# One barrier per stage, earlier gathers in the mixture with capacity, and mixture sums written into the output tensor

## The reference

```python
C = int(CAP_FACTOR * S / E)                      # 160 rows for each expert
h = relu(einsum('ecd,edh->ech', xin, w1) + b1)   # xin: the rows picked for expert e
out = einsum('ech,ehd->ecd', h, w2) + b2
final = zeros.at[idx.reshape(-1)].add(out * weight)
```

```python
x = x + _L3_ffn_ref(_layernorm(x, axis=-1), L3_ffn_Wg, L3_ffn_bg, ...)
return x
```

## Time and profile before

| | us |
|---|---|
| median of 3 runs (lowest, highest) | 1863.27 (1859.93, 1864.88) |
| the profiled execution's own time | 1854.92 |
| its span, first to last instruction | 1852.8 |
| mean granted clock of TensorE | 0.939 |

### The profile page before, as it was taken

One profiled execution on the slowest core, in us unless ns is written; L12 is line 12 of the kernel. 1 busy time (PEld: TensorE's weight loads), 2 busy tenths in 40 slices (PEclk: granted clock), 3 DMA queues, 4 the chain that ended last, 5 costly groups with the idle time before them and its releaser, 6 DMA issues. The chain is left out here.

```text
span 1852.8 us, 35956 instructions
## 1 busy us (share of the span) xinstructions
PE 1617.7 (87%) x12777; PEld 1376.1 (74%) x12777; DVE 1109.5 (60%) x3057; ACT 817.1 (44%) x2383; POOL 792.2 (43%) x934
## 2 busy tenths in 40 slices
PE   6999999766887999987899999969959888859997
PEld 5899989634556999965798889845648745548996
DVE  5888786468854888845666766728951132363331
ACT  4766666213324888831666666620003212113332
POOL 7656656253337999833111111116732420102332
PEclk9999999789897999998999999989969989979998
DMA  8554554200013343302533333251036285761222
GB/s 257 176 169 152 175 164 153 79 1 1 1 28 121 137 139 124 130 18 90 162 107 113 115 106 114 82 187 36 1 103 205 30 210 138 253 218 36 37 40 46
DMA packets 139520, 206.20 MB, mean 111 GB/s; under 512 B 21410, under 2 KB 107106, under 8 KB 138706
## 3 DMA queue, kind: packets, MB, share of 16 engines
q1 hardware_dynamic: 131922, 194.07, 32.8%
q0 software_dynamic: 6720, 8.79, 3.0%
q10 hardware_dynamic: 704, 1.05, 0.2%
HBM read 163.53 MB, written 42.19 MB: 111 GB/s over the span
## 5 line engine op out<-in xcount | busy, mean ns | idle before, releaser
L810 DVE TENSOR_SCALAR xattn_oT<-bank,xattn_last 128x256 f32<-128x256 f32 x256 | 111.8, 478 | 91.7 <-PE bank L631 91.7
L716 ACT ACTIVATE xattn_probs<-bank,xattn_negmax 128x257 f32<-128x257 f32 x256 | 123.7, 483 | 65.5 <-DVE xattn_negmax L791 65.4
L721 ACT ACTIVATE xattn_probs<-xattn_probs,xattn_rsum 128x257 f32<-128x257 f32 x256 | 131.9, 515 | 1.4 <-DVE xattn_rsum L795 1.4
L1036 POOL TENSOR_SCALAR xattn_probs<-xattn_probs,xattn_rsum 128x257 f32<-128x257 f32 x128 | 119.5, 933 | 23.6 <-DVE xattn_rsum L1273 23.5
L791 DVE TENSOR_REDUCE xattn_negmax<-bank 128x1 f32<-128x257 f32 x256 | 106.5, 416 | 34.8 <-PE bank L604 33.2
L800 DVE TENSOR_TENSOR xattn_probsT_lo<-bank,xattn_probsT_hi 128x256 fp32r<-128x256 f32 x256 | 105.1, 410 | 9.8 <-ACT xattn_probsT_hi L727 8.7
L611 PE MATMUL bank<-ident,xattn_probs 128*128 128x128 f32 x512 | 103.9, 285 | 7.0 <-ACT xattn_probs L721 6.5
L147 ACT COPY xnT<-bank 128x512 f32<-128x512 f32 x40 | 21.4, 590 | 200.6 <-PE bank L137 200.6
L727 ACT CAST xattn_probsT_hi<-bank 128x256 fp32r<-128x256 f32 x256 | 95.4, 373 | 32.3 <-PE bank L611 28.2
L549 POOL COPY ctx_stat<-xattn_mv 128x2 f32<-128x2 f32 x32 | 6.0, 188 | 237.9 <-DVE xattn_mv L824 237.9
L600 PE MATMUL bank<-xattn_ctxT,xattn_qk_hi 128*128 128x258 f32 x256 | 93.8, 367 | 0.5 <-DVE xattn_qk L787 0.5
(11 more groups left out here) (488 smaller groups left out, 5332.6 us busy)
## 6 DMA issues: line engine op xcount, KB each, us to landing
xattn_ctxT<-ctx_partsT SPq DMA_DIRECT2D x64, 516.0 KB, 4.0
xattn_ctxN<-ctx_partsN SPq DMA_DIRECT2D x64, 384.0 KB, 4.2
ctx_partsT<-xattn_ctxT SPq DMA_DIRECT2D x32, 516.0 KB, 2.6
moe_w<-in_L_ffn_W SPq DMA_DIRECT2D x16, 1024.0 KB, 12.9
ctx_partsN<-xattn_ctxN SPq DMA_DIRECT2D x32, 384.0 KB, 3.5
moecap_w_early<-in_L_ffn_w SPq DMA_DIRECT2D x10, 1024.0 KB, 9.3
xattn_rawN<-in_ctx SPq DMA_DIRECT2D x32, 192.0 KB, 2.7
xattn_raw<-in_ctx SPq DMA_DIRECT2D x32, 192.0 KB, 4.3
```

Source lines behind the costliest of these rows:

```text
L716: nc.scalar.activation(probs[:, n % RING, :], SB[n % 2][:, 0:KV], ACT.Exp, bias=negmax[:, n % RING:n % RING + 1], accum_out=psum[:, n % RI ...
L721: nc.scalar.mul(probs[:, n % RING, :], probs[:, n % RING, :], rsum[:, n % RING:n % RING + 1]).then_inc(norm_ready, 1)
L810: nc.vector.tensor_scalar(oT[k][:, heads, b, :], by_head(OB[:, k * 2 * P:(k + 1) * 2 * P]), last[:, k, j * PER_TILE + b:j * PER_TILE + b + ...
L1036: nc.gpsimd.tensor_scalar(probs[:, n % RING, :], probs[:, n % RING, :], rsum[:, n % RING:n % RING + 1], None, ALU.mult).then_inc(norm_read ...
```

## The change

Three edits.

1. The second barrier of a stage's end goes. Instead, the semaphore numbers of the ended stage rest for one more stage: they are cleared by POOL, reserved again under new names, and released only when the following stage has ended. So a number comes into use again only after another block's barrier has passed.
2. In the mixture with capacity POOL issues one gather more ahead of its sums: gathers 0 to 3 first, then gather(n + 4) and add(n).
3. The last mixture's sums are accumulated in the output tensor itself, which is made P = 128 rows longer (the spare rows of padding; the host takes the first 1024). The eight copies and the wait for them go. SP still waits for all sums.

```diff
     def end(self):
-        self.core.nc.clear_and_free_semaphores(self.sems)
-        self.core.nc.all_engine_barrier()
+        core, nc = self.core, self.core.nc
+        nc.clear_and_free_semaphores(self.sems)
+        for rested in core.resting:
+            nc.release_semaphore(rested)
+        core.resting = [nc.alloc_semaphore(f"{self.name}_rests{k}", num=sem.num) for k, sem in enumerate(self.sems)]
...
-        self.sum = nc.dram_tensor(f"{name}_sum", (TOKENS + spare, D), F32, kind="Internal").ap()
+        self.sum = sums if sums is not None else nc.dram_tensor(f"{name}_sum", (TOKENS + spare, D), F32, kind="Internal").ap()
...
-            for n in range(XS):
+            for n in range(XS + 1):
                 gather(n)
             for n in range(E):
-                if n + XS < E:
-                    gather(n + XS)
+                if n + XS + 1 < E:
+                    gather(n + XS + 1)
                 add(n)
...
-        self.rows = Rows(core, ctx, "moe", self.E, P)
+        self.rows = Rows(core, ctx, "moe", self.E, P, core.out)
...
-        def put_out(eng, tiles):
-            for z in range(YS):
-                eng.wait_ge(y_added[z], 16 * len(range(z, BLOCKS, YS)))
-            for t in tiles:
-                eng.dma_start(out[t * P:(t + 1) * P, :], rows.sum[t * P:(t + 1) * P, :]).then_inc(put, 16)
...
-            put_out(sp, range(0, TILES, 2))
-            sp.wait_ge(put, TILES * 16)
+            for z in range(YS):
+                sp.wait_ge(y_added[z], 16 * len(range(z, BLOCKS, YS)))
...
-            put_out(act, range(1, TILES, 2))
...
-    out = nc.dram_tensor("out_0_dram", (BATCH, SEQ, D), F32, kind="ExternalOutput").ap()
+    out = nc.dram_tensor("out_0_dram", (TOKENS + P, D), F32, kind="ExternalOutput").ap()
```

More of the change, by code:

```diff
@@ L30, in __init__ @@
         self.nc, self.dram = nc, dram
+        self.resting = []
         self.x = ctx.enter_context(nc.sbuf_tensor("x", [P, TILES, D], F32))
@@ L2378, with __init__ @@
 class Rows:
-    def __init__(self, core, outer, name, experts, spare):
+    def __init__(self, core, outer, name, experts, spare, sums=None):
         nc = core.nc
@@ L2777, in stage_moe @@
         y_added = [st.sem(f"y_added{k}") for k in range(YS)]
-        put = st.sem("put")
         steps = st.sem("dve_steps")
         block = ctx.enter_context(nc.Block())
-        out = core.out.rearrange("b s n -> (b s) n")
         def expert_of(eng, n):
             return eng.value_load(expert_u[0:1, n:n + 1], min_val=0, max_val=E - 1)
-        def put_out(eng, tiles):
-            for z in range(YS):
-                eng.wait_ge(y_added[z], 16 * len(range(z, BLOCKS, YS)))
-            for t in tiles:
-                eng.dma_start(out[t * P:(t + 1) * P, :], rows.sum[t * P:(t + 1) * P, :]).then_inc(put, 16)
         @block.sync
@@ L3506 @@
         dram[name] = nc.dram_tensor(f"in_{name}", a.shape, _mybir.dt.from_np(a.dtype), kind="ExternalInput").ap()
-    out = nc.dram_tensor("out_0_dram", (BATCH, SEQ, D), F32, kind="ExternalOutput").ap()
+    out = nc.dram_tensor("out_0_dram", (TOKENS + P, D), F32, kind="ExternalOutput").ap()
     program(nc, dram, out)
     r = _run(nc, [arrays], core_ids=[0])
-    return r.results[0]["out_0_dram"]
+    return r.results[0]["out_0_dram"][0:TOKENS].reshape(BATCH, SEQ, D)
```

## The result

| | before | after |
|---|---|---|
| median of 4 runs each, us (lowest, highest) | 1861.77 (1859.93, 1864.88) | 1829.39 (1827.55, 1832.97) |
| ratio, 95% interval | | 0.9827 (0.9803 to 0.985) |
| the profiled execution's own time | 1854.92 | 1831.08 |
| its span | 1852.8 | 1829.2 |
| mean granted clock of TensorE | 0.939 | 0.948 |

From profile to profile the gain is 23.8 us, against 15.2 forecast.

What follows compares the result with a forecast made beforehand. PE, busy 87% of the span, was taken as the bound, so only its standstills and stage ends could be won: 7.4 + 3.3 + 4.5 = 15.2 us, from 1863.3 to 1848, range 1842 to 1856.

Steps and rivals of the forecast that it cites:

- Barrier: At the eleven stage ends inside the kernel, removing the second barrier saves 7.4 us.
- the twelfth: Second barrier at the kernel's end, about 0.6 us, counted within the 4.5 us saved there.
- The cover of POOL's clears: At stage starts, DVE's statistics run 1.78 us before POOL's first work, hiding clears of typically 0.7 us.
- The rival that the first barrier absorbs the second: At stage ends, fetches, clears or loads show instead: only 7.8 us saved in all, 1855.5; chance 0.06.
- Gathers: In the mixture with capacity, earlier gathers close PE's idle hole before expert 4, saving 3.3 us.
- no other wait took its place: Lower bound of the saving at expert 4: 0 us if PE meets another wait there.
- Output: At the kernel's end, dropping the copies moves the end from 1852.8 to 1848.3, saving 4.5 us.
- POOL's DRAIN holds the end: At the last barrier POOL arrives last, its DRAIN of 5.83 us running to 1847.4.
- The sum: Over the whole kernel, 7.4 + 3.3 + 4.5 = 15.2 us saved.
- The clock eats it: At stage starts, four more low-clock starts cost 11.6 us, leaving a gain of 3.6, 1859.7; chance 0.04.
- no PE idle time grows, all shrink: Argument over all PE idle stretches against a loss of 11.6 us through the lower clock.
- The base: Whole-kernel starting time for the subtraction: the runs' median, 1863.3 us, instead of the profiled execution's 1854.9.

Runs made afterwards that it cites:

- e2_barrier_only: Kernel before with only the second barrier removed at all stage ends; median 1843.41 us, ratio 0.9926.
- e13: Kernel before with the second barrier removed at all stage ends except the scan's; median 1847.77 us, ratio 0.9959.
- e4_output_only: Kernel before with only the last mixture's sums moved into the output tensor and the copies gone, both barriers kept; median 1851.56 us, ratio 0.9979.
- e9: Kernel after with the second barrier put back at the scan's end only; median 1837.88 us, ratio 0.9893.
- e10: Kernel before with the second barrier removed at the scan's end only; median 1855.09 us, ratio 0.9986.
- e15: Kernel after, unchanged, measured a third time in six executions; median 1837.64 us, ratio 0.9896 against the kernel before.
- the control: Kernel before run once more, nothing changed; median 1858.32 us, ratio 1.0007.
- e11: Kernel after with both barriers put back at all ends, leaving the earlier gathers and the output sums; median 1847.08 us, ratio 0.9948.
- e5: Kernel after, unchanged, measured again in six executions; median 1832.13 us, ratio 0.9878 against the kernel before.
- e8: Kernel before with one more barrier, three instead of two, at each of its twelve ends; median 1858.0 us, ratio 1.0005.
- e14: Kernel before, all barriers kept, with 24 useless matmuls ahead of the first transposes of the mixture with capacity; median 1850.39 us, ratio 0.9964.

## Why the prediction was wrong

**Barrier (7.4, with the twelfth 8.0): right.** 8.5 at equal clock in `e2_barrier_only`, 6.3 in e13, which has it at eleven ends. The cover of POOL's clears held in the profile after. The rival that the first barrier absorbs the second is refuted.

**Gathers (3.3): right.** 3.7 at equal clock; the hole is gone and no other wait took its place.

**Output (4.5): right.** 4.6 in the profile. POOL's DRAIN holds the end as worked out, with 6.4 us from the last issue where 6.5 had been given; the sums land as before in 3.8. That the twelfth second barrier is part of the 4.5 didn't show: with it (`e4_output_only`) and without it the span ends 6.4 us behind the last sum's issue. The kernel after has a second DRAIN and clear there instead.

**The sum: right for what it counts.** 15.2 forecast, 15.4 at equal clock over sixteen executions.

**The step that failed is the clock.** The sum priced every matmul at its old duration. The rival "The clock eats it" let the clock move in one direction only, and the line against it ("no PE idle time grows, all shrink") was an argument for a gain, which neither the range nor a rival took up. The clock went from .9405 to .9464, and 22.9 less 15.4, that is 7.5 us, came with it; up to 1.4 of these, by the estimate above, are the tail at 0.50 that is gone, and no faster matmul. Of that, 3.0 us are shown at one place, the gate matmuls behind the scan's end (e9, e10). About 1.25 us more stand in the profile at the up matmuls of expert 0 (7.41 before, 6.16 after), but these took 7.5 in `e2_barrier_only` and 7.4 in e15, so they aren't tied to an edit. Where the remaining 3 to 4 us arise isn't settled. One reason is that the profiles of one kernel differ by as much in single stages: that of L3015 took 99.1 us before and 95.6 in the control, and 96.2, 94.6 and 99.4 in the three profiles of the kernel after. The first stage, which no edit can reach, ends at 353.9 in e11 too, with both barriers kept.

**The base was off by chance.** The sum was subtracted from the median of three executions, 1863.3, though the profiled one had 1854.9; over 102 executions the mean is 1856.5. And the four executions of the first measurement of the kernel after were 4 us under its mean of sixteen. So the 18.7 us between 1848.1 and 1829.4 are 6.8 of base, 7.7 of a larger gain (22.9 less 15.2) and 4.2 of chance in the kernel after. The range took the runs' spread as 2 to 4 us, while single executions of this kernel scatter over 23.

## What to carry to other kernels

A change that lets a stage's matmuls start half a microsecond earlier can be worth several times that, or nothing, by which clock level the matmuls behind it meet. So add to the sum a term for the clock with both signs: go through the stretches where PE is fully busy at 0.50 behind an idle stretch, and price the matmuls there at both levels. And before a difference under 1% is taken at its number, relate the executions' times to their granted clocks, with the kernel before run some tens of times; here the parts could only be read after that.

## What was not expected of the hardware

- The level that the gate matmuls behind the scan's end meet is the same in every profile of a kernel, although a thousand microseconds of work lie ahead: 6.83 or 6.84 us in nine profiles with two or three barriers there, 3.7 to 4.1 in five with one. (Of one and the same kernel there are two profiles before and three after; the others differ in edits elsewhere.) In the last mixture the same kind of matmuls is by chance in one or the other: 3.95, 6.83 and 3.73 us in the three profiles of the kernel after (the first, e5, e15). The Trainium skill (page "TensorE: Matmul & The Clock Gate", section "What's actually happening") says that how many matmuls run at the lower level varies from run to run of the same kernel. The trace agrees for the last mixture and disagrees for the scan's end, where it came out alike each time.
- A barrier of all engines costs 0.33 us when nobody is late, and 0.57 where it also waits for a clear of 0.17.
- Behind the hole at expert 4 the down matmuls ran partly at the lower level in three profiles (e8, e10 and e14: 6.19, 5.67 and 6.19 us) and at the upper one (4.51) in all others that have the hole. A hole in TensorE's work can so cost 1.2 to 1.7 us more than its own length, and the same hole in another build nothing more. These three holes were the longest of the nine (3.52, 3.90 and 3.64 us; 3.33 in the kernel before).
